# Two-layer attention network on one core: in the first layer, values kept by head, attended tokens split during attention, output projection begun in the drain, four early groups

## The reference, cut to what matters

```python
x_norm = group_norm(x_flat) * scale + bias            # 32 groups of 16 channels
qkv = x_norm @ w_qkv + b_qkv                          # 512 -> 1536
q, k, v = split(qkv)                                  # 8 heads of 64 channels
weight = softmax(einsum('bhld,bhsd->bhls', q * scale, k * scale))
out = einsum('bhls,bhsd->bhld', weight, v)
out = out @ w_out + b_out
return x_flat + out
```

## Time and profile before

| | us |
|---|---|
| median of 3 runs | 4412.85 (4411.47 to 4413.67) |
| profiled execution | 4408.6 |
| its span, first to last instruction | 4406.9 |
| PE busy | 4119.7 (93%) |
| DVE busy | 3071.6 (70%) |
| ACT busy | 2523.8 (57%) |
| POOL busy | 1313.1 (30%) |
| mean granted TensorE clock | 0.975 of full speed |

### The profile page before, as it was taken

One profiled execution on the slowest core, in us unless ns is written; L12 is line 12 of the kernel. 1 busy time (PEld: TensorE's weight loads), 2 busy tenths in 40 slices (PEclk: granted clock), 3 DMA queues, 4 the chain that ended last, 5 costly groups with the idle time before them and its releaser, 6 DMA issues. The chain is left out here.

```text
span 4406.9 us, 65281 instructions
## 1 busy us (share of the span) xinstructions
PE 4119.7 (93%) x22762; PEld 3415.9 (78%) x22762; DVE 3071.6 (70%) x5125; ACT 2523.8 (57%) x5486; POOL 1313.1 (30%) x1423
## 2 busy tenths in 40 slices
PE   7999989989999999899999899999999898989998
PEld 6977978978878879789788577777777776767777
DVE  3983965947839839659478368677686867676867
ACT  3864845837828638558377146464646363645545
POOL 1432423422324314234234004041323223140404
PEclk9999999999999999999999899999999999999999
DMA  2221221221212212212211302030303121212212
GB/s 79 49 66 32 55 64 28 58 59 29 68 39 46 66 35 49 70 28 58 58 39 39 118 23 84 26 86 15 96 20 78 39 58 58 58 58 48 68 33 64
DMA packets 113184, 236.20 MB, mean 54 GB/s; under 512 B 17260, under 2 KB 33704, under 8 KB 112808
## 3 DMA queue, kind: packets, MB, share of 16 engines
q1 hardware_dynamic: 112808, 231.41, 19.6%
HBM read 80.35 MB, written 33.55 MB: 26 GB/s over the span
## 5 line engine op out<-in xcount | busy, mean ns | idle before, releaser
L560 DVE TENSOR_REDUCE a_neg_max<-a_ps 128x1 f32<-128x1024 f32 x512 | 626.2, 1224 | 396.3 <-PE a_ps L443 396.3
L577 DVE TENSOR_TENSOR a_pl<-a_ps,a_ph 128x512 fp32r<-128x512 f32 x1024 | 655.0, 680 | 11.6 <-ACT a_ph L519 8.3
L519 ACT ACTIVATE a_ph<-a_ps 128x512 fp32r<-128x512 f32 x1024 | 555.1, 593 | 188.2 <-PE a_ps L454 185.1
L526 ACT ACTIVATE a_prob<-a_ps,a_neg_max 128x1024 f32<-128x1024 f32 x512 | 572.7, 1118 | 20.5 <-DVE a_neg_max L560 20.5
L1562 POOL TENSOR_SCALAR b_prob<-b_prob,b_row_inv 128x256 f32<-128x256 f32 x512 | 247.6, 484 | 1049.2 <-DVE b_row_inv L1480 1013.3
L427 PE MATMUL a_ps<-a_ph,a_v 128*128 128x256 f32 x2048 | 550.7, 302 | 0.0
L640 POOL TENSOR_TENSOR a_qk<-a_fold_s,a_fold_r 64x256 f32<-64x256 f32 x256 | 188.4, 736 | 1213.1 <-DVE a_fold_s L568 1213.1
L454 PE MATMUL a_ps<-a_ident,a_prob 128*128 128x128 f32 x4096 | 534.4, 273 | 10.0 <-DVE a_pl L577 10.0
L454 PEld LDWEIGHTS a_ps<-a_ident,a_prob 128*128 128x128 f32 x4096 | 474.9, 140 | 86.9 <-issue 19.3
L427 PE MATMUL a_ps<-a_pl,a_v 128*128 128x256 f32 x2048 | 509.3, 282 | 0.0
L442 PE MATMUL a_ps<-a_kh,a_qs 128*128 128x512 f32 x1024 | 410.4, 401 | 31.2 <-ACT a_prob L526 13.0
(11 more groups left out here) (246 smaller groups left out, 9340.7 us busy)
## 6 DMA issues: line engine op xcount, KB each, us to landing
a_qs<-a_qk SPq DMA_DIRECT2D x128, 256.0 KB, 4.3
a_kl<-a_qk SPq DMA_DIRECT2D x128, 256.0 KB, 4.4
a_xtok<-in_x SPq DMA_DIRECT2D x64, 256.0 KB, 4.4
a_tok<-in_x SPq DMA_DIRECT2D x64, 256.0 KB, 4.4
x<-a_tok SPq DMA_DIRECT2D x64, 256.0 KB, 2.0
b_xs<-x SPq DMA_DIRECT2D x64, 256.0 KB, 4.9
b_qs<-b_qh SPq DMA_DIRECT2D x64, 256.0 KB, 3.0
b_qs<-b_ql SPq DMA_DIRECT2D x64, 256.0 KB, 3.8
```

The costliest lines, as they stand in the source:

```text
L519: act.activation(ph[:, b % 2, 4 * g:4 * g + 4, (u % 2) * P:(u % 2 + 1) * P], ps[:, 4 + n % 2, :].rearrange("p (k q) -> p k q", k=4), ACT.C ...
L526: act.activation(prob[:, i_ % 2, :], ps[:, 2 * (i_ % 2):2 * (i_ % 2) + 2, :] .rearrange("p a b -> p (a b)"), ACT.Exp, bias=neg_max[:, i_:i ...
L560: dve.tensor_reduce(neg_max[:, i_:i_ + 1], ps[:, 2 * (i_ % 2):2 * (i_ % 2) + 2, :] .rearrange("p a b -> p (a b)"), AX, ALU.max, negate=Tru ...
L577: dve.tensor_tensor(pl[here], ps[:, 4 + n % 2, :].rearrange("p (k q) -> p k q", k=4), raw(ph[here]), ALU.subtract).then_inc(pl_ok, 1)
```

## The change

- **Values by head.** `v` is now [head][token tile][high, low]: a head's values are one slot of 4 KB per partition, free once the head is done. `v_hi` and `v_lo` go; sizes of the instructions stay.
- **Splits during attention.** `a2` puts chunk c (heads 2c and 2c + 1) of the attended tokens into the slots of its own two heads; the low part of the last chunk goes where the even heads' keys were staged. `SPLIT_AT` sets the iterations: 128x512 pieces of chunks 0, 1, 2 in iterations 23, 25, 39, 41, 55, 57, and four 128x256 pieces of chunk 3 in 64, 66, 68, 70, at the end of the iteration's work on ACT and DVE.
- **Start of attention.** `LATE` = 2: scores 0 and 1 come before the last two projection groups on PE; ACT evicts these two behind exponentials 0 and 1. The waits for all evictions move to the first transpose and the first product with values.
- **Drain.** Two tiles of the next image are turned in each of iterations 65 and 66; output tile 0 is computed between the two halves of the last block's product, tile 1 behind it, then tiles 4 to 7 of the next image are turned.
- **Early groups.** `EARLY` = 4, computed chunk by chunk: 12 matmuls when a chunk's high and low parts are ready. The group average moves from behind output tile 2 to behind tile 3.
- **DVE's tail** is written out: residual 0 between the two halves of the statistics, residuals 1 and 2 ahead of the variance, each low part soon behind its normalisation.
- **Token loads.** The residual tiles get other places (`tok_a`, `tok_b`); SP issues tiles 0 and 1 after the last scores, 2 to 5 after the last transposes, 6 and 7 after the last product.

```diff
-        v = R.take("a_v", [P, TT, NH * P], F32R)
+        v = R.take("a_v", [P, NH, TT, P], F32R)
...
-        ah = S.take("a_ah", [P, CT, TOK], F32R)
-        al = S.take("a_al", [P, CT, TOK], F32R)
+        a2 = Region(nc, v_at, v_at + 28672).take("a_a2", [P, 2 * CT - 1, TOK], F32R)
+        al_last = Region(nc, work - 8192, work - 4096).take("a_al_last", [P, TOK], F32R)
+        ah = [a2[:, 2 * c, :] for c in range(CT)]
+        al = [a2[:, 2 * c + 1, :] for c in range(CT - 1)] + [al_last]
...
-        AVERAGE_AT = 2
+        AVERAGE_AT = 3
+        SPLIT_AT = {16 * c + 23 + 2 * s: (c, slice(s * HALF, (s + 1) * HALF)) for c in range(CT - 1) for s in range(2)}
+        SPLIT_AT.update({U + 2 * j: (CT - 1, slice(256 * j, 256 * j + 256)) for j in range(NB)})
+        SPLITS = 2 * (CT - 1)
...
-        EARLY = 2
+        EARLY = 4
+        LATE = 2
+        def early(pe):
+            for k in range(CT):
+                pe.wait_ge(xh_ok, k + 1)
+                pe.wait_ge(xl_ok, k + 1)
+                for g in range(EARLY):
+                    project(pe, g, (k,))
...
+                    def out_tile(t):
+                        if t == 0:
+                            pe.wait_ge(pl_ok, 2 * U - 1)
+                        elif t == 1:
+                            pe.wait_ge(pl_ok, 2 * U)
+                        elif t in (2, 3):
+                            pe.wait_ge(fold_add, U // 2 + t - 3)
+                            pe.wait_ge(fold_cp, U + 2 * (t - 3))
+                        else:
+                            pe.wait_ge(out_ok, t - 3)
...
+                    projections(range(EARLY, len(groups) - LATE))
+                    scores(0)
+                    scores(1)
+                    projections(range(len(groups) - LATE, len(groups)))
+                    for i_ in range(2, U + 5):
+                        if i_ >= 5:
+                            output((i_ - 5) // 2, (i_ - 5) % 2)
+                        if i_ < U:
+                            scores(i_)
+                        if i_ < U + 2:
+                            transposes(i_ - 2)
+                        if i_ in (U + 1, U + 2):
+                            turn(range(2 * (i_ - U - 1), 2 * (i_ - U)))
+                        if i_ == U + 3:
+                            out_tile(0)
+                    out_tile(1)
+                    turn(range(4, TT))
+                    for t in range(2, TT):
+                        out_tile(t)
...
+                        if i_ in SPLIT_AT:
+                            c, n = SPLIT_AT[i_]
+                            act.wait_ge(att_ok, 2 * NB * (c + 1) if c < CT - 1 else U // 2 - NB + (i_ - U) // 2 + 1)
+                            act.activation(ah[c][:, n], qk[:, c, n], ACT.Copy).then_inc(ah_ok, 1)
...
+                        if i_ in SPLIT_AT:
+                            c, n = SPLIT_AT[i_]
+                            dve.wait_ge(ah_ok, list(SPLIT_AT).index(i_) + 1)
+                            dve.tensor_tensor(al[c][:, n], qk[:, c, n], raw(ah[c][:, n]), ALU.subtract)\
+                               .then_inc(al_ok, 1)
...
+                        dve.wait_ge(xt_sb, 4)
+                        stats(dve, 0)
+                        residual(0)
+                        dve.wait_ge(xt_sb, 8)
+                        stats(dve, 1)
+                        moments(dve, link)
+                        residual(1)
+                        residual(2)
+                        variance(dve, link)
+                        affine(dve, link)
+                        normalise(dve, 0).then_inc(xn_ok, 1)
+                        normalise(dve, 1).then_inc(xn_ok, 1)
+                        split(0)
+                        residual(3)
```

More of the change, by code:

```diff
@@ L320, in _ @@
                 pe.wait_ge(wql_ok, CT)
[L321 to L324 removed]
+                early(pe)
             @block.vector
@@ new lines, in output @@
+                    def output(b, part):
+                        h = b // NB
+                        if part == 0:
+                            pe.wait_ge(inv_ok, b + 1)
+                            if b == 0:
+                                pe.wait_ge(vl_ok, n_v)
+                            if b >= 2:
+                                pe.wait_ge(fold_add, b - 1)
+                                pe.wait_ge(fold_cp, 2 * b - 2)
+                            for n in range(2):
+                                u = 2 * b + n
+                                pe.transpose(ps[:, 6 + b % 2, 256 + n * P:256 + (n + 1) * P],
+                                             row_inv[:, u:u + 1].to_broadcast([P, P]), ident[:])
+                        pe.wait_ge(pl_ok, 4 * b + 3 + part)
+                        for kt in range(4 * part, 4 * part + 4):
+                            for e, q_ in enumerate((ph, pl)):
+                                mm = pe.matmul(ps[:, 6 + b % 2, 0:256], v[:, h, kt, :], q_[:, b % 2, kt, :],
+                                               start=kt == 0 and e == 0, stop=kt == TT - 1 and e == 1)
+                        if part == 1:
+                            mm.then_inc(av_ps, 1)
@@ L497, in _ @@
                                            bias=vec[:, 8 + m:9 + m]).then_inc(qk_sb, 1)
+                    for g in range(len(groups) - LATE):
+                        evict(g)
                     for i_ in range(U + 7):
@@ new lines, in split @@
+                    def split(c):
+                        dve.wait_ge(xh_ok, c + 1)
+                        low(dve, c).then_inc(xl_ok, 1)
+                    if after is None:
+                        for t in range(TT):
+                            residual(t)
+                    else:
+                        dve.wait_ge(xt_sb, 4)
[12 more added lines that the diff above has]
+                        residual(3)
+                        normalise(dve, 2).then_inc(xn_ok, 1)
+                        split(1)
+                        residual(4)
+                        normalise(dve, 3).then_inc(xn_ok, 1)
+                        split(2)
+                        residual(5)
+                        split(3)
+                        residual(6)
+                        residual(7)
```

187 lines of the change are left out of this document (67 added, 120 removed).

## The result

The changed kernel takes **4336.22 us** (median of 4 runs, 4335.97 to 4337.14); the kernel before, in the same session, 4412.16 us (4 runs, 4408.43 to 4413.67). The ratio is 0.983, with a 95% interval of 0.9812 to 0.9847: 76 us, 1.7%, faster.

A forecast was written before the change was run, and what follows sets the result against it. The prediction took PE to bound projection and attention, and nothing for long the tail, costing everything as PE time. Terms -21.6 + 38.4 - 53.2 - 6 - 1 gave -43.4 us: 4365.2 profiled, 4369 against the median, range 4346 to 4392.

The forecast's parts named there:

- start of attention: Score tiles 0 and 1 ahead of the last two projection groups remove two PE waits: 2.7 us won an image, 21.6 in all.
- splits in attention: Six 128x512 pairs in attention make DVE's row maximum late; PE loses 1.6 us a pair of iterations, 38.4 in all.
- tail, seven images: Reordered tail with output tiles 0 and 1 in the drain and 48 early matmuls: 7.6 us won an image, 53.2 in all.
- tail, last image: In the last image's tail, without a next image, losses of 2.83 and about 3.3 us go: minus 6 us.
- first early groups: The very first early groups no longer wait for the last low part: minus 1 us.
- Rival 1: Splits in attention are absorbed but for 0.3 us each: 14 us lost instead of 38.4, total 4345; chance 0.12.
- 0.8 + 0.3 + 2.3 + 1.6: PE's tail losses: before turning tiles 4 to 7, at the average, before output tile 7, then half clock; sum 5.0 us.
- the second way of adding up: Tail gain as old losses of 11.9 us less new losses of 5.0: 6.9 us an image, beside 7.6 from end times.
- The tail bound by DVE's chain: Statistics or residual 3 late by 3 to 4 us more; 4 us an image won, 25 us worse, 4394; chance 0.17.
- The slower case: Attention's subtraction meets POOL's staging and takes 1.75 us, delaying row maxima: 51 us worse, 4421; chance 0.05.
- the groups only cross the barrier: The two further early groups only move across the barrier as the gap grows: 38 us lost, 4407, no difference; chance 0.04.
- A longer attention stage than 181 us: Sign that the forecast was wrong: attention stage longer than 175.9 + 4.8 us.

## Why the prediction was wrong in size, point by point

The measured terms, from PE's timelines of before and after:

| term | predicted | measured | how |
|---|---|---|---|
| start of attention | −21.6 | −23 | 2.9 x 8 |
| splits in attention | +38.4 | +20 | 2.45 x 8, by leaving them out |
| tail, seven images | −53.2 | −61 | 58.2 − 55.0 + 5.44 = 8.65 each, last score to next start |
| tail, last image | −6 | −6.6 | 38.61 to 32.05, last score to last output matmul |
| first early groups | −1 | −1.2 | 40.76 to 45.01, less 5.44 |
| sum | −43.4 | −72 | the first layer gained 73.6 |

**Start of attention: right**, mechanism and size. Both waits of the earlier trace rows went, and score tile 2 stands directly behind the projection. Leaving out the late groups gave back 1.83 us an image, the wait for the exponential.

**Splits: right in mechanism, mis-sized; this is the step that failed.** The sentence was "PE loses 1.05" for iteration 25 and 0.55 for iteration 23, 1.6 a pair; measured are 0.6 and 0.2, 0.8 a pair: 19.6 us in place of 38.4. The lateness had two terms and the slack was a third, and each was taken to PE's cost. First, the copy was put behind the end of ACT's read of the accumulator; it starts 0.09 after the read's start (466.10 and 466.19). Second, the subtraction was counted with its duration, 0.68; the next maximum starts 0.61 behind it (466.85 and 467.46). Together the maximum is late by 0.9, not 1.2: it stands 1.34 behind the start of the reciprocal (466.12 and 467.46), against 0.42 in the kernel without splits (468.00 and 468.42). Third, the slack was taken as 0.15, from the old pair's end against the load's start; 0.9 late gives 0.6 lost, so some 0.3 was there. The text ahead of the prediction warned that matmul durations are longer than pitches; the prediction then used durations for DVE and ACT. 19 of the 33 us missed lie here. Rival 1, the splits absorbed but for 0.3 us each, had a price of 14 us: the measured 20 is nearer to it than to the forecast, and the copy one iteration earlier shows how to absorb the rest.

**Tail: the order and the waits right, the clock wrong.** All three waits were met within 0.1 us, and the early matmuls stood gapless. The losses named were 0.8 + 0.3 + 2.3 + 1.6; the 1.6 at half clock behind the new wait was carried over from the old wait of 2.73 us and came in one image of seven, which is 9 to 10 us. Nothing in the rows of before could say in which images it comes: there it had followed the 2.73 us wait in six of seven. The gap at the barrier, taken as unchanged, went from a mean of 5.3 us to 4.8, 3 us in all; why is not settled. Against these, PE's last early matmul came 0.7 us an image later than the forecast chain would give at full clock, from small differences along it. Per image that is 1.4 + 0.4 − 0.7 = 1.1, seven times. That the sum for the tail came within 8 us is thus partly luck, since the 0.7 hid half of the missing half clock. And one of the old losses was read too high: the wait before old tile 6 was 0.60 us in this image (PE at 623.72), not 0.8. It enters only the second way of adding up.

**Rest.** About 2 us were won at the projections' first matmuls at half clock, which I had left alone. And the 4.25 us by which the profiled execution of before lay under its median were added to the forecast; the change's profiled execution lies at its median, so they were not there: against the profiled 4408.6 the change gained 72.5, against the median 76. The second layer gave back 1.1.

**Rivals.** The tail bound by DVE's chain with 25 us less won did not happen, though DVE's chain is what the 2.2 us wait hangs on. The slower case, the subtraction beside POOL's staging at 1.75 us, did not happen: 48 subtractions at 0.69, all where POOL is idle. The trace of the change therefore does not test the rule of the Trainium skill (SBUF — State Buffer, Who interferes with whom) in attention; in the tail it agrees, where the last quarter split starts beside a running addition of POOL's and takes 1.145 us in seven images and 1.165 in the last, against a median of 0.426. The two middle quarter splits, which start 0.1 us ahead of POOL's product, keep their 0.426. That the groups only cross the barrier is true of the two further groups by themselves: moving them wins nothing but for the half clock (two early groups). The gap behind the barrier did not grow, though, and the gain of the tail stayed.

**What was to show it.** Score tile 2 behind the projection, gaps at six places named for L577's successor (L616), a gap near 2.3 before tile 7, 48 early matmuls gapless: all seen; the gaps were 0.3 to 0.6, not 0.5 and 1.0. "A longer attention stage than 181 us" was the sign against me, on a stage that starts behind score tile 2 (175.88 in the earlier trace rows); it did not come, since from score tile 2 on the stage grew by 2.4 us, to 178.3. From the first score the splits' price does not show: 181.1 before and 187.0 less the 5.44 moved in, 181.6, because the gain at the start nearly cancels it.

## What to carry to other kernels

Where two engines share a split, issue the first engine's half one step ahead of the second's: the wait of the second in its queue, not its work, is what reached the bound engine (here 2.4 us an image). Work placed in a gap of the bound engine must not stand ahead of what the longest chain behind it starts from: output tile 0 in the drain covered nothing and held up everything, and behind the last product it filled a wait. When lateness is passed from engine to engine, sum it in start-to-start times of the trace, not in durations, and price the slack by taking work out or doubling it.

## What the runs showed of the hardware

- **The clock behind a wait of 2.2 us** differs from kernel to kernel. The same 2.19 to 2.20 us wait before output tile 7 is followed by half clock (1.2 GHz, some eight matmuls 0.43 apart, 1.6 us lost) in 1 image of 7 with four early groups, in 7 with two, in 6 without late groups, in 4 with all chunks waited for, in 3 with the doubled subtraction, in 2 with the copy one iteration earlier and in 2 with the splits left out; each of the two kernels that were run twice had the same count in its second profile. The 2.73 us wait of before had it in 6 of 7, a 2.91 us wait in 2, the 3.12 us waits of the kernel that waits for all chunks in 3 of 3; behind waits of 1.57 us (output tile 0 behind the last product) none of seven had it. What decides between the images is open. Between the change and the kernel with two early groups, which do the same work, it is 9.6 of the 10.5 us.
- **ACT's read of the accumulator is nearly free.** It has a duration of 0.20 us, but the copy behind it starts 0.09 behind its start (a fold copy, L544, starts 0.22 behind it). The Trainium skill (ScalarE: Activation LUTs, What ACT_TABLE_LOAD costs) says that back-to-back ACTIVATEs overlap by about 93 ns; this trace agrees, with 0.10 us between the two halves of L558. Here the copy starts at 466.19, 0.03 before the exponential's end at 466.22, with the read between them, so 0.07 of ACT's time is an estimate of what the read takes.
- **Small DVE instructions beside POOL.** In the change's tail a 128x4 product of two SBUF tiles that starts just ahead of POOL's additions (605.00 to 610.49) takes 0.16 us, and the next one, which starts inside them, 1.16, seven times as much. It ends 0.02 us behind the addition that was running when it started (606.31 and 606.29), and so does the step behind it (607.56 and 607.54): as if each had to wait for the rest of POOL's instruction. Both stand in the chain to the normalisation:

```profile
604.96 0.16 DVE L223 TENSOR_TENSOR a_small<-a_small,a_vec 128x4 f32<-128x4 f32 x1 [1.20 <-POOL a_small L709]
605.15 1.16 DVE L224 TENSOR_TENSOR a_small<-a_small 128x4 f32<-128x4 f32 x1
...
605.00 2.54 POOL L705 TENSOR_TENSOR a_tok_a<-a_tok_a,a_bout 128x512 f32<-128x512 f32 x2
```

That is 2 us of that chain (L224 and the step behind it) which no run here tried to take out; the two normalisations beside POOL, 1.74 and 1.79 us against 0.80 for the two behind them, cost another 1.9.
